# Seven slots instead of eight for the exponentials, a flat fan-out of the reciprocals, and the output bias added by TensorE, in a fused attention and feed-forward kernel

## The chip, the cores and the metric

The program runs on the 8 cores of one Trainium2 chip. Cores 2b and 2b+1 share batch b: each owns 2048 of its 4096 rows and reads the other 2048 for keys and values. The cores don't talk to each other. The metric is the device time of the slowest core, in microseconds (us). Before the change it was 1568.64 us, the median of three runs (1566.05 to 1570.06).

## The reference

```python
x = x + attention(layernorm(x), query_proj, key_proj, value_proj, output_proj)   # x: 4 x 4096 x 1024
x = x + ffn(layernorm(x), Win, bin_, W1, b1, W2, b2, Wout, bout)

# attention: 16 query heads of 64, one key head and one value head shared by all
q = einsum('bnd,hkd->bnhk', r, query_proj); k = r @ key_proj; v = r @ value_proj
attn = softmax(q k / sqrt(64)); out = einsum('bnhv,dhv->bnd', attn v, output_proj)

# ffn, 64 narrow units of inner width 16
s = x @ Win + bin_;  h = relu(s[..., None] * W1 + b1);  g = sum(h * W2) + b2;  out = g @ Wout + bout
```

## The kernel before

Five queues of instructions, one for each engine, are filled by calls of `S.emit` in program order; each call names the semaphore values that it waits for. The order of these calls is the order on each engine. A wait that the same engine has already passed is not repeated.

**Stage A** (the first 262 us) loads weights, normalises 32 tiles of 128 rows, transposes them and makes keys `k2t`, values `vab` and queries `qt`.

**Stage B** is attention. It goes through 1024 groups in one row: 4 blocks k of 512 queries, in each 8 pairs of heads, in each 32 chunks `mc` of 128 keys. For a group TensorE makes the scores of both heads (`s_pair`, line 479: two matmuls, one on array rows 0 to 63 and one on 64 to 127) into one of two PSUM buffers `spa` and `spb`, ScalarE takes the exponential of all 128x1024 of them into a slot of `ptu` (line 494), and TensorE multiplies four quarters of it with the values (line 518, here called PV). In turn `it` of the loop the queues get: the exponential of group `it`; the scores of group `it + 2`; and four PV matmuls, into `oAe` for group `it - 5`, `oAo` for `it - 4`, `oBe` for `it - 3` and `oBo` for `it - 2`. So the last reader of a group's slot runs in the turn five later. The scores of a group wait for the exponential of the group two before, which frees their PSUM buffer. `pvT[g]` is the semaphore value that the last PV of turn `g + 2` gives.

With eight slots, the slot of group g was last read in turn g - 3. The scores of group g come later than that on TensorE's queue, so the exponential's wait for its own scores covers it, and there is no other wait.

At the end of each pair of heads VectorE copies `oBo` and `oAo` to `big` (line 533) and adds `oBe` and `oAe` (line 536). The ones column of `vab` gives the softmax sums, gathered in `zstage`. At the end of a block k the sums of 16 heads are inverted (line 566) and written to DRAM as 64 copies of a 16x512 table, `zscr`: SyncE writes four copies (line 572), then doubles them four times, 4 to 8 to 16 to 32 to 64 (line 576), each doubling waiting for the one before. GpSimd reads 64 copies of a head's row into 64 partitions (`rcpb`, line 587), and VectorE multiplies (`emit_zmult`, line 432). For blocks 0 to 2 these products are queued on VectorE in the pairs of heads of the next block, from the 11th chunk of each; for the last block they stand at the start of stage C.

**Stage C** projects the heads (`op_ps`, line 733), adds x (line 708), spills the sum to DRAM (`x2d`, line 753), normalises and transposes. After every fourth tile `emit_D` does the feed-forward of 512 rows: eight rounds of Relu and multiply-add, then for each of four tiles `fo = g2b @ wout2b` (line 659), a load of the spilled tile (`big<-x2d`, line 667), their sum (line 670), the bias (line 678) and two half stores (line 682). There is one `fo`. SyncE's queue holds load, store, store, load, store, store, so a load stands behind the stores of the tile before it.

Of the kernel before, what the change touches and what calls it, by code (L numbers as in the profile page):

```python
# [7 lines left out]
F32 = mybir.dt.float32  # L8
BF16 = mybir.dt.bfloat16
AF = mybir.ActivationFunctionType  # L10
# [12 lines left out]
EPS = 1e-5  # L23

ENGS = ("sync", "tensor", "vector", "scalar", "gpsimd")
SEMS = ("pe", "dve", "act", "xa", "xb", "xc", "xd", "g", "zg", "zs", "zs2", "zs3", "zs4", "out", "ou2", "ou3", "ou4", "wd", "od", "zh", "pl", "x2r")
DMA_SEMS = {"xa", "xb", "g", "zg", "zs", "out"}


# [55 lines left out]
def build_nc(debug=False, upto='D'):  # L85
# [4 lines left out]
    nc = bass.Bass("TRN2", target_bir_lowering=False)  # L90
# [38 lines left out]
    st = contextlib.ExitStack()  # L129
    with st:  # L130
# [7 lines left out]
        boutbc = st.enter_context(nc.sbuf_tensor("boutbc_s", [128, D], F32))  # L138
        stats = st.enter_context(nc.sbuf_tensor("stats", [128, 8, 4], F32))
        w1p = st.enter_context(nc.sbuf_tensor("w1p_s", [128, 8], F32))  # L140
        b1p = st.enter_context(nc.sbuf_tensor("b1p_s", [128, 8], F32))
        b1adj = st.enter_context(nc.sbuf_tensor("b1adj", [128, 8], F32))
        w2p = st.enter_context(nc.sbuf_tensor("w2p_s", [128, 8], F32))
        bin2 = st.enter_context(nc.sbuf_tensor("bin2_s", [128, 1], F32))
        b2h = st.enter_context(nc.sbuf_tensor("b2h_s", [128, 1], F32))
# [5 lines left out]
        wout2b = st.enter_context(nc.sbuf_tensor("wout2b", [128, D], BF16))  # L151
        identb = st.enter_context(nc.sbuf_tensor("identb", [128, 128], BF16))
        k2t = st.enter_context(nc.sbuf_tensor("k2t", [128, NFULL], BF16))
        vab = st.enter_context(nc.sbuf_tensor("vab", [128, MC, 65], BF16))
        qt = st.enter_context(nc.sbuf_tensor("qt", [128, DCH, NOWN], BF16))
        ot = st.enter_context(nc.sbuf_tensor("ot", [128, DCH, NOWN], BF16))
        r1t = st.enter_context(nc.sbuf_tensor("r1t", [128, 2, DCH, NTW], BF16))
        ptu = st.enter_context(nc.sbuf_tensor("ptu", [128, 8, 1024], BF16))
        r1u = st.enter_context(nc.sbuf_tensor("r1u", [128, 2, D], BF16))
        g2b = st.enter_context(nc.sbuf_tensor("g2b", [128, NTW], BF16))  # L160

# [2 lines left out]
        S = Sched(block, sems)  # L164
# [5 lines left out]
        def x2dbuf(q):  # L170
            return big[:, 4096 + q * 1024: 4096 + (q + 1) * 1024]
        def obuf(q):
            return big[:, 6144 + q * 1024: 6144 + (q + 1) * 1024]
# [93 lines left out]
        for dsrc, ddst in direct:  # L267
# [73 lines left out]
        for step in range(NTILES + 3):  # L341
# [4 lines left out]
            if i < NTILES:  # L346
                q = i % 4
# [14 lines left out]
            if 0 <= i < NTILES:  # L362
                q, qr = i % 4, i % 2
# [8 lines left out]
            if 0 <= i < NTILES:  # L372
# [4 lines left out]
                    waits=[("pe", trans_t[i]), ("pe", slabmm_t.get(i // 4 - 2, 0))], inc="dve")  # L377
# [28 lines left out]
        sp = [spa, spb]  # L406
# [45 lines left out]
        sPT = {}  # L452
        pvT = {}
# [33 lines left out]
        for it in range(-2, NG + PVLAG):  # L487
            gmc = it
            if 0 <= gmc < NG:
                ew = [("pe", sPT[gmc])]  # L490
                if first_act:
                    ew += bwB["scalar"]
                    first_act = False
                expT[gmc] = S.emit("scalar", lambda s_, gmc=gmc: s_.activation(  # L494
                    ptu[:, gmc % 8, :], sp[gmc % 2][:], AF.Exp, scale=0.125),
                    waits=ew, inc="act")
            gmc = it + 2
            if 0 <= gmc < NG:
# [8 lines left out]
            for oi in range(4):  # L507
# [8 lines left out]
                if mc == 0:  # L516
                    w_i.append(("dve", tcfree.get((hp - 1, oi), 0)))
                tgt = S.emit("tensor", lambda te, ob=ob, rg=rg, col=col, mc=mc, gmc=gmc: te.matmul(  # L518
                    ob[:], vab[rg:rg + 64, mc, :], ptu[rg:rg + 64, gmc % 8, col:col + 512],
                    start=(mc == 0), stop=(mc == MC - 1)),  # L520
                    waits=w_i, inc="pe" if (oi == 3 or mc == MC - 1) else None)
                if oi == 3:
# [24 lines left out]
            if 0 <= gmc < NG:  # L547
                k, j, mc = gmc // (NHP * MC), (gmc // MC) % NHP, gmc % MC
                hp = gmc // MC
                if mc == MC - 1:  # L550
                    tg = None
                    if j == NHP - 1 and KHP == NHP and os.environ.get("KNTEND") != "0":
# [18 lines left out]
                        for cc in range(4):  # L571
                            tzo = S.emit("sync", lambda e, cc=cc: e.dma_start(zscr[cc], recipz[:]),
                                         waits=tzw if cc == 0 else (), inc="zh", inc_n=16)
                        for dd in range(2, 6):
                            lo, hi = 1 << dd, 1 << (dd + 1)
                            tzo = S.emit("sync", lambda e, lo=lo, hi=hi: e.dma_start(
                                zscr[lo:hi], zscr[0:lo]),
                                waits=[("zh", tzo)], inc="zh", inc_n=16)

                        def emit_bcast(kk, i_, tzo=tzo):  # L580
                            zst = zstate[kk]
# [34 lines left out]
        r2evac_t = {}  # L616
        tfa_t = {}
        out_r = out_d.rearrange("(t p) d -> t p d", p=128)
        spill_t = {}
        r2norm_t = {}  # L620
        relu_t = {}
# [6 lines left out]
        def emit_D(k):  # L628
# [25 lines left out]
            for ns in range(4):  # L654
                t = k * 4 + ns
                q = ns % 2
                fw = [("dve", tg2b), ("dve", fadd_t.get(t - 1, 0))]
                for half in range(2):
                    fo_mm_t[t] = S.emit("tensor", lambda te, ns=ns, half=half: te.matmul(  # L659
                        fo[:, half * 512:(half + 1) * 512], g2b[:, ns * 128:(ns + 1) * 128],  # L660
                        wout2b[:, half * 512:(half + 1) * 512], start=True, stop=True),
                        waits=fw if half == 0 else (), inc="pe" if half == 1 else None)
                sm = "wd" if t % 2 == 0 else "x2r"
                osems = ("out", "ou3") if t % 2 == 0 else ("ou2", "ou4")
                xw = [("g", spill_t[t]), ("dve", tfa_t.get(t - 2, 0)),
                      ("dve", multT.get((KL, HEADS - 1), 0))]
                txl = S.emit("sync", lambda e, t=t, q=q: e.dma_start(
                    x2dbuf(q), x2d.rearrange("(t p) d -> t p d", p=128)[t]),
                    waits=xw, inc=sm, inc_n=16)
                tfa = S.emit("vector", lambda v, q=q: v.tensor_tensor(  # L670
                    obuf(q), x2dbuf(q), fo[:], op=ALU.add),
                    waits=[("pe", fo_mm_t[t]), (sm, txl),
                           (osems[0], outdma_t.get((t - 2, 0), 0)),
                           (osems[1], outdma_t.get((t - 2, 1), 0)),
                           ("dve", multT.get((KL, HEADS - 1), 0))],
                    inc="dve")
                tfa_t[t] = tfa
                fadd_t[t] = S.emit("vector", lambda v, q=q: v.tensor_tensor(  # L678
                    obuf(q), obuf(q), boutbc[:], op=ALU.add),
                    waits=[("dve", tfa)], inc="dve")  # L680
                for h in range(2):
                    outdma_t[(t, h)] = S.emit("sync", lambda e, t=t, q=q, h=h: e.dma_start(
                        out_r[t, :, h * 512:(h + 1) * 512], obuf(q)[:, h * 512:(h + 1) * 512]),
                        waits=[("dve", fadd_t[t])] if h == 0 else (), inc=osems[h], inc_n=16)

        KL = KNT - 1
        for step in range(16 + 4):
# [146 lines left out]
```

How the kernel before makes its waits and increments, by code:

```python
            def body(e, items=items):  # L74
                for waits, fn, inc, inc_n in items:
                    for s, v in waits:
                        e.wait_ge(self.sems[s], v)
                    r = fn(e)
                    if inc is not None:
                        r.then_inc(self.sems[inc], inc_n)
```

## Time and profile before

| | |
|---|---|
| median of three runs | 1568.64 us |
| the profiled execution | 1568.78 us |
| its span, slowest core (0) | 1567.2 us |
| spans of the 8 cores | 1551.0 to 1567.2 us |
| ScalarE busy | 1104.5 us (70%) |
| TensorE busy, matmul | 1097.0 us (70%) |
| VectorE busy | 358.9 us (23%) |
| mean granted clock of TensorE, core 0 | 0.88 |

The span is what lies between the first and the last instruction of the program on the slowest core. The granted clock is 1 at 2.4 GHz and 0.5 at 1.2 GHz. Matmul ends are modelled, and busy times of pipelined instructions overlap, so a busy share near 1 doesn't mean that an engine works at its peak. A name such as `DMA zscr<-zscr` in the chain is a transfer from its issue to its landing.

### The profile page before, as it was taken

Reading aid. Unit: us, or ns where it says so; the run is one execution under the profiler, and the core shown is the slowest. Engines: PE = TensorE matmul, PEld = TensorE weight load, DVE = VectorE, ACT = ScalarE, POOL = GpSimd, SP = SyncE. Lnnn points to the kernel's source line nnn. Section 1 sums busy time; section 2 is a strip of 40 time slices with the busy share of each in tenths; the row PEclk is TensorE's granted clock in tenths of the full one; section 3 lists DMA queues with packets and bytes.
Section 4 is the critical chain, followed back from the end, with each engine's and each line's share of the span. In section 5 each row is a group of like instructions: output and inputs, shape, how many; then the busy total and the mean of one; then the engine's idle time right before and its main releaser. Section 6 shows DMA issues by size and latency. Waiting matters only on the chain.

```text
span 1567.2 us, 20849 instructions; the slowest of 8 cores (1551.0 to 1567.2 us)
## 1 busy us (share of the span) xinstructions
PE 1097.0 (70%) x7407; PEld 417.6 (27%) x7424; DVE 358.9 (23%) x663; ACT 1104.5 (70%) x1347; POOL 94.8 (6%) x188
## 2 busy tenths in 40 slices
PE   0376646999999889999899999889999345253421
PEld 0233322333333233333333333333333112021110
DVE  2344443101001211211211111121121134343443
ACT  0523354999999899999899999989999214040310
POOL 0000000000000100100110000010000030000000
PEclk9987766999999999999999999999999768575755
DMA  5311232100000200000200000200000142325132
GB/s 163 121 56 57 82 111 82 43 1 1 1 1 1 85 10 10 18 3 3 77 18 10 9 12 3 62 27 16 10 10 4 54 144 98 129 86 178 63 134 94
DMA packets 30227, 81.74 MB, mean 52 GB/s; under 512 B 9264, under 2 KB 10288, under 8 KB 29872
## 3 DMA queue, kind: packets, MB, share of 16 engines
q1 hardware_dynamic: 21424, 60.87, 11.9%
q0 software_dynamic: 8704, 19.54, 3.9%
q8 instruction: 63, 1.03, 0.3%
q14 instruction: 36, 0.29, 0.1%
HBM read 60.34 MB, written 25.17 MB: 55 GB/s over the span
## 4 chain that ended last, share of the span: by engine, by line
ACT 43%; PE 19%; DMA 16%; issue 11%; DVE 9%; SPq 1%; DVEq 0%; POOL 0%; ACTq 0%; POOLq 0%
ACT ptu L494 37%; DMA zscr<-zscr 4%; DMA x2d<-big 4%; PE qps L332 4%; DMA big<-x2d 3%; PE spa L479 3%; PE oAe L518 3%; PE oBe L518 3%; PE spb L479 2%; ACT big L189 2%; ACT big L185 2%; PE kps L305 2%; DMA ot<-r1u 1%; DVE big L678 1%; DVE big L670 1%
## 5 line engine op out<-in xcount | busy, mean ns | idle before, releaser
L494 ACT ACTIVATE ptu<-spb 128x1024 bf16<-128x1024 f32 x512 | 568.6, 1110 | 15.2 <-PE spb L479 14.7
L494 ACT ACTIVATE ptu<-spa 128x1024 bf16<-128x1024 f32 x512 | 569.6, 1113 | 1.5 <-PE spa L479 1.4
L518 PE MATMUL oBo<-ptu,vab 64*65 64x512 bf16 x1024 | 389.2, 380 | 14.9 <-DVE big L533 12.4
L518 PE MATMUL oAo<-ptu,vab 64*65 64x512 bf16 x1024 | 387.9, 379 | 2.5 <-DVE big L533 0.5
L518 PE MATMUL oBe<-ptu,vab 64*65 64x512 bf16 x1024 | 386.9, 378 | 1.4
L518 PE MATMUL oAe<-ptu,vab 64*65 64x512 bf16 x1024 | 384.8, 376 | 2.0 <-DVE big L536 0.4
L479 PE MATMUL spa<-qt,k2t 64*128 64x512 bf16 x1024 | 205.0, 383 | 48.3 <-ACT ptu L494 6.3
L479 PE MATMUL spb<-qt,k2t 64*128 64x512 bf16 x1024 | 211.0, 383 | 38.8 <-ACT ptu L494 0.5
L533 DVE COPY big<-oBo 65x512 f32<-65x512 f32 x32 | 22.0, 687 | 722.5 <-PE oBo L518 722.2
L202 ACT ACTIVATE stats<-stats,epsb 128x1 f32<-128x1 f32 x48 | 14.1, 294 | 225.9 <-DVE stats L200 225.9
L518 PEld LDWEIGHTS oBe<-ptu,vab 64*65 64x65 bf16 x1024 | 108.7, 106 | 98.0 <-issue 14.7
L479 PEld LDWEIGHTS spa<-qt,k2t 64*128 64x128 bf16 x1024 | 65.0, 93 | 254.5 <-issue 251.7
L479 PEld LDWEIGHTS spb<-qt,k2t 64*128 64x128 bf16 x1024 | 65.5, 93 | 242.9 <-issue 239.9
L220 PE MATMUL trpsA<-identb,r1u 128*128 128x128 bf16 x256 | 30.1, 291 | 135.2 <-DVE r1u L210 135.2
L518 PEld LDWEIGHTS oAo<-ptu,vab 64*65 64x65 bf16 x1024 | 119.6, 117 | 17.9 <-issue 17.7
L518 PEld LDWEIGHTS oBo<-ptu,vab 64*65 64x65 bf16 x1024 | 110.8, 108 | 29.7 <-issue 29.6
L518 PEld LDWEIGHTS oAe<-ptu,vab 64*65 64x65 bf16 x1024 | 106.8, 104 | 20.0 <-issue 16.2
L733 PE MATMUL op_ps<-wq_wp,ot 128*128 128x512 bf16 x248 | 77.4, 477 | 47.9 <-DVE ot L432 35.3
L659 PE MATMUL fo<-wout2b,g2b 128*128 128x512 bf16 x32 | 16.2, 608 | 101.2 <-DVE big L678 67.0
L540 POOL DMA_DIRECT2D zstage<-big x64 | 31.7, 496 | 813.7 <-DVE big L536 745.4
L185 ACT ACT_TABLE_LOAD x2 | 2.6, 1283 | 96.3 <-DVE ot L432 53.8
L220 PEld LDWEIGHTS trpsA<-identb,r1u 128*128 128x128 bf16 x256 | 22.9, 130 | 142.6 <-issue 142.6
(63 smaller groups left out, 778.0 us busy)
## 6 DMA issues: line engine op xcount, KB each, us to landing
xbuf<-x_own SPq DMA_DIRECT2D x32, 512.0 KB, 3.6
xbuf<-x_oth SPq DMA_DIRECT2D x16, 512.0 KB, 3.3
rcpb<-zscr POOLq DMA_DIRECT2D x64, 128.0 KB, 2.7
x2d<-big POOLq DMA_DIRECT2D x16, 512.0 KB, 2.9
big<-x2d SPq DMA_DIRECT2D x16, 512.0 KB, 4.1
out<-big SPq DMA_DIRECT2D x32, 256.0 KB, 2.3
xbuf<-wq SPq DMA_DIRECT2D x8, 512.0 KB, 4.3
xbuf<-wp SPq DMA_DIRECT2D x8, 512.0 KB, 4.2
```

Of the source, the lines that this page charges most:

```text
L185: "scalar", lambda s, a=xt_ap, dmp=dmp, c=sc: s.activation(dmp, a, AF.Square, accum_out=stat(SUMSQ, c)),
L189: "scalar", lambda s, a=xt_ap, dmp=dmp, c=sc: s.activation(dmp, a, AF.Identity, accum_out=stat(SUMS, c)),
L220: t = S.emit("tensor", lambda te, jj=jj, h=half: te.transpose(trps[:, h * 1024 + jj * 128: h * 1024 + (jj + 1) * 128], src_ap_fn(jj), iden ...
L305: t = S.emit("tensor", lambda te, j=j: te.matmul(kps[:], wkb[:, j, :], R1T[:, j, :], start=(j == 0), stop=(j == DCH - 1)), waits=mmw if j ...
L332: t = S.emit("tensor", lambda te, j=j, c=c: te.matmul(qps[:, c % 2, :], wq_wp[:, j, c * 128:(c + 1) * 128], R1T[:, j, :], start=(j == 0), ...
L479: tgt = S.emit("tensor", lambda te, mc=mc, rg=rg, hh=hh, j=j, k=k: te.matmul(sp[gmc % 2][:, hh * 512:(hh + 1) * 512], k2t[rg:rg + 64, mc * ...
L494: expT[gmc] = S.emit("scalar", lambda s_, gmc=gmc: s_.activation(ptu[:, gmc % 8, :], sp[gmc % 2][:], AF.Exp, scale=0.125), waits=ew, inc=" ...
L518: tgt = S.emit("tensor", lambda te, ob=ob, rg=rg, col=col, mc=mc, gmc=gmc: te.matmul(ob[:], vab[rg:rg + 64, mc, :], ptu[rg:rg + 64, gmc % ...
L533: tcfree[(hp, oi)] = S.emit("vector", lambda v, hi=hi, hh=hh: v.tensor_copy(tv(hi)[0:65, :], obank[2 * hh + 1][:]), waits=tw, inc="dve")
L540: tg = S.emit("gpsimd", lambda e, hi=hi: e.dma_start(zstage[hi:hi + 1, :], tv(hi)[64:65, :]), waits=[("dve", tc)] + (bwB["gpsimd"] if hp = ...
L659: fo_mm_t[t] = S.emit("tensor", lambda te, ns=ns, half=half: te.matmul(fo[:, half * 512:(half + 1) * 512], g2b[:, ns * 128:(ns + 1) * 128] ...
L733: tmm = S.emit("tensor", lambda te, t=t, half=half, c=c: te.matmul(op_ps[:, t % 2, half * 512:(half + 1) * 512], ot[:, c, t * 128:(t + 1) ...
```

## The change

Four edits:

1. `ptu` has seven slots. The exponential of group g now waits as well for `pvT[g - 4]`, the last PV of turn g - 2.
2. The fan-out of `zscr`: after the four first copies, 15 transfers of four copies each, all from the first four, with one wait ahead of the first. The bytes are the same.
3. The bias goes into `fo` on TensorE: after each half's bf16 matmul one of a [1, 128] row of ones with the fp32 bias row. VectorE's bias addition is gone, the stores wait for the sum of line 670, and the next tile's `fo` waits for that too.
4. The load of the spilled tile is cut into two halves with a semaphore each.

```diff
-        ptu = st.enter_context(nc.sbuf_tensor("ptu", [128, 8, 1024], BF16))
+        ptu = st.enter_context(nc.sbuf_tensor("ptu", [128, 7, 1024], BF16))
+        S.emit("vector", lambda v: v.memset(ones1[:], 1.0))
...
-                ew = [("pe", sPT[gmc])]
+                ew = [("pe", sPT[gmc]), ("pe", pvT.get(gmc - 4, 0))]
...
-                        for dd in range(2, 6):
-                            lo, hi = 1 << dd, 1 << (dd + 1)
-                            tzo = S.emit("sync", lambda e, lo=lo, hi=hi: e.dma_start(
-                                zscr[lo:hi], zscr[0:lo]),
-                                waits=[("zh", tzo)], inc="zh", inc_n=16)
+                        seed = tzo
+                        for rr in range(1, 16):
+                            tzo = S.emit("sync", lambda e, rr=rr: e.dma_start(
+                                zscr[4 * rr:4 * rr + 4], zscr[0:4]),
+                                waits=[("zh", seed)] if rr == 1 else (), inc="zh", inc_n=16)
...
-                fw = [("dve", tg2b), ("dve", fadd_t.get(t - 1, 0))]
+                fw = [("dve", tg2b), ("dve", tfa_t.get(t - 1, 0))]
...
-                        wout2b[:, half * 512:(half + 1) * 512], start=True, stop=True),
-                        waits=fw if half == 0 else (), inc="pe" if half == 1 else None)
+                        wout2b[:, half * 512:(half + 1) * 512], start=True, stop=False),
+                        waits=fw if half == 0 else ())
+                    fo_mm_t[t] = S.emit("tensor", lambda te, half=half: te.matmul(
+                        fo[:, half * 512:(half + 1) * 512], ones1[:],
+                        boutbc[0:1, half * 512:(half + 1) * 512], start=False, stop=True),
+                        inc="pe" if half == 1 else None)
...
-                txl = S.emit("sync", lambda e, t=t, q=q: e.dma_start(
-                    x2dbuf(q), x2d.rearrange("(t p) d -> t p d", p=128)[t]),
-                    waits=xw, inc=sm, inc_n=16)
+                for h in range(2):
+                    txl[h] = S.emit("sync", lambda e, t=t, q=q, h=h: e.dma_start(
+                        x2dbuf(q)[:, h * 512:(h + 1) * 512],
+                        x2d_r[t, :, h * 512:(h + 1) * 512]),
+                        waits=xw if h == 0 else (), inc=rsems[h], inc_n=16)
...
-                fadd_t[t] = S.emit("vector", lambda v, q=q: v.tensor_tensor(
-                    obuf(q), obuf(q), boutbc[:], op=ALU.add),
-                    waits=[("dve", tfa)], inc="dve")
...
-                        waits=[("dve", fadd_t[t])] if h == 0 else (), inc=osems[h], inc_n=16)
+                        waits=[("dve", tfa)] if h == 0 else (), inc=osems[h], inc_n=16)
```

In stage B no instruction changes its place. This is TensorE's queue after the change, one turn of the loop and the start of the next (`L481` is the scores' line, `L520` that of PV, both two lines lower than before):

```order
L481 MATMUL spa<-qt,k2t 128x512 [waits sem_act]
L481 MATMUL spa<-qt,k2t 128x512
L520 MATMUL oAe<-ptu,vab 65x512
L520 MATMUL oAo<-ptu,vab 65x512
L520 MATMUL oBe<-ptu,vab 65x512
L520 MATMUL oBo<-ptu,vab 65x512
L481 MATMUL spb<-qt,k2t 128x512 [waits sem_act]
```

The exponential that reads `spa` waited for the second of these rows; now it waits for the sixth.

SyncE's queue at the end of block 0, before (`recipz` is the table of inverted sums):

```order
L572 DMA zscr<-recipz 16x512 [waits sem_dve]
L572 DMA zscr<-recipz 16x512 x3
L576 DMA zscr<-zscr 16x2048 [waits sem_zh]
L576 DMA zscr<-zscr 16x4096 [waits sem_zh]
L576 DMA zscr<-zscr 16x8192 [waits sem_zh]
L576 DMA zscr<-zscr 16x16384 [waits sem_zh]
```

And after:

```order
L574 DMA zscr<-recipz 16x512 [waits sem_dve]
L574 DMA zscr<-recipz 16x512 x3
L578 DMA zscr<-zscr 16x2048 [waits sem_zh]
L578 DMA zscr<-zscr 16x2048 x14
```

Four waits have become one, and four transfers 15 of the smallest size.

TensorE's queue for two tiles of `emit_D` after the change (`L662` is what was line 659, `L666` the bias; `ones` is the row of ones):

```order
L662 MATMUL fo<-wout2b,g2b 128x512 [waits sem_dve]
L666 MATMUL fo<-boutbc_s,ones 128x512
L662 MATMUL fo<-wout2b,g2b 128x512
L666 MATMUL fo<-boutbc_s,ones 128x512
L662 MATMUL fo<-wout2b,g2b 128x512 [waits sem_dve]
```

A tile had two matmuls here and has four; the wait of the last row is now for the sum of the tile before, no longer for the bias addition behind it.

## Rows read from the trace of the kernel before

**Rows 1.** The exponentials into one buffer: duration ns min/median/max, first and last start us.
```profile
L494 ACT ACTIVATE ptu<-spb x512: 1017/1106/1197, 264.9 to 1224.9; 128x1024 bf16<-128x1024 f32 x171
```

**Rows 2.** Timeline, one turn in steady state: start us, us, engine, line, op, tiles, count.
```profile
799.21 1.03 ACT L494 ACTIVATE ptu<-spa 128x1024 bf16<-128x1024 f32 x1
...
800.38 0.39 PE L479 MATMUL spa<-qt,k2t 64*128 64x512 bf16 x2
...
800.83 0.38 PE L518 MATMUL oBo<-ptu,vab 64*65 64x512 bf16 x1
...
801.02 1.05 ACT L494 ACTIVATE ptu<-spa 128x1024 bf16<-128x1024 f32 x1
```

**Rows 3.** Timeline, start of stage B, at the lower clock; in brackets idle time and releaser.
```profile
268.90 0.61 PE L479 MATMUL spa<-qt,k2t 64*128 64x512 bf16 x2
...
269.73 0.63 PE L518 MATMUL oBo<-ptu,vab 64*65 64x512 bf16 x1
269.82 0.97 PE L479 MATMUL spb<-qt,k2t 64*128 64x512 bf16 x2
...
270.89 1.02 ACT L494 ACTIVATE ptu<-spb 128x1024 bf16<-128x1024 f32 x1 [0.26 <-PE spb L479]
```

**Rows 4.** Timeline where block 1's first pair of heads ends.
```profile
533.52 1.20 ACT L494 ACTIVATE ptu<-spa 128x1024 bf16<-128x1024 f32 x1
536.10 0.68 DVE L432 TENSOR_TENSOR ot<-big,rcpb 64x512 bf16<-64x512 f32 x1 [23.31 <-DMA rcpb<-zscr]
...
537.49 0.69 DVE L533 COPY big<-oBo 65x512 f32<-65x512 f32 x1
538.32 0.60 PE L518 MATMUL oBo<-ptu,vab 64*65 64x512 bf16 x1 [4.49 <-DVE big L533]
...
539.45 1.02 ACT L494 ACTIVATE ptu<-spb 128x1024 bf16<-128x1024 f32 x1 [4.73 <-PE spb L479]
```

**Rows 5.** Chain of waits after the last block: start us, us, what.
```profile
1238.81 4.08 DMA zscr<-zscr
...
1249.72 7.65 DMA zscr<-zscr
...
1257.91 2.68 DMA rcpb<-zscr
```

**Rows 6.** Timeline, the four tiles of the first feed-forward block.
```profile
1337.24 1.01 PE L659 MATMUL fo<-wout2b,g2b 128*128 128x512 bf16 x2 [8.53 <-DVE g2b L652]
1338.43 1.22 DVE L670 TENSOR_TENSOR big<-big,fo 128x1024 f32<-128x1024 f32 x1 [1.33 <-PE fo L659]
...
1341.05 0.82 SPq L682 DMA_DIRECT2D out<-big  x2
...
1341.96 0.41 SPq L667 DMA_DIRECT2D big<-x2d  x1
1346.06 1.22 DVE L670 TENSOR_TENSOR big<-big,fo 128x1024 f32<-128x1024 f32 x1 [5.08 <-DMA big<-x2d]
...
1361.87 1.22 DVE L670 TENSOR_TENSOR big<-big,fo 128x1024 f32<-128x1024 f32 x1 [5.20 <-DMA big<-x2d]
...
1364.33 0.81 DVE L210 TENSOR_SCALAR ptu<-big,stats 128x1024 bf16<-128x1024 f32 x1
```

**Rows 7.** The page's DMA issues: queue, count, size of each, median us to landing.
```profile
big<-x2d SPq DMA_DIRECT2D x16, 512.0 KB, 4.1
out<-big SPq DMA_DIRECT2D x32, 256.0 KB, 2.3
```

**Rows 8.** Stretches: window, length, busy us of each engine, granted clock, DMA share, GB/s.
```profile
1319.80:1333.50 13.70, 7.51 (x39) 3.25 (x38) 7.05 (x14) 9.31 (x16) 0.53 (x1) 1.00 0.10 39
...
1333.50:1371.00 37.50, 9.76 (x28) 3.15 (x29) 13.97 (x18) 2.40 (x5) 0.53 (x1) 0.50 0.40 132
...
800.00:1000.00 200.00, 180.37 (x1300) 63.64 (x1296) 29.73 (x41) 199.60 (x218) 14.32 (x28) 1.00 0.03 9
```

More of the change, by code:

```diff
@@ L25 @@
 ENGS = ("sync", "tensor", "vector", "scalar", "gpsimd")
-SEMS = ("pe", "dve", "act", "xa", "xb", "xc", "xd", "g", "zg", "zs", "zs2", "zs3", "zs4", "out", "ou2", "ou3", "ou4", "wd", "od", "zh", "pl", "x2r")
+SEMS = ("pe", "dve", "act", "xa", "xb", "xc", "xd", "g", "zg", "zs", "zs2", "zs3", "zs4", "out", "ou2", "ou3", "ou4", "wd", "od", "zh", "pl", "x2r", "x2b", "x2c")
 DMA_SEMS = {"xa", "xb", "g", "zg", "zs", "out"}
@@ L142, in build_nc @@
         b1adj = st.enter_context(nc.sbuf_tensor("b1adj", [128, 8], F32))
+        ones1 = st.enter_context(nc.sbuf_tensor("ones1", [1, 128], F32))
         w2p = st.enter_context(nc.sbuf_tensor("w2p_s", [128, 8], F32))
@@ L494, in build_nc @@
                 expT[gmc] = S.emit("scalar", lambda s_, gmc=gmc: s_.activation(
-                    ptu[:, gmc % 8, :], sp[gmc % 2][:], AF.Exp, scale=0.125),
+                    ptu[:, gmc % 7, :], sp[gmc % 2][:], AF.Exp, scale=0.125),
                     waits=ew, inc="act")
@@ L518, in build_nc @@
                 tgt = S.emit("tensor", lambda te, ob=ob, rg=rg, col=col, mc=mc, gmc=gmc: te.matmul(
-                    ob[:], vab[rg:rg + 64, mc, :], ptu[rg:rg + 64, gmc % 8, col:col + 512],
+                    ob[:], vab[rg:rg + 64, mc, :], ptu[rg:rg + 64, gmc % 7, col:col + 512],
                     start=(mc == 0), stop=(mc == MC - 1)),
@@ L618, in build_nc @@
         out_r = out_d.rearrange("(t p) d -> t p d", p=128)
+        x2d_r = x2d.rearrange("(t p) d -> t p d", p=128)
         spill_t = {}
@@ L656, in emit_D @@
                 q = ns % 2
-                fw = [("dve", tg2b), ("dve", fadd_t.get(t - 1, 0))]
+                fw = [("dve", tg2b), ("dve", tfa_t.get(t - 1, 0))]
                 for half in range(2):
-                    fo_mm_t[t] = S.emit("tensor", lambda te, ns=ns, half=half: te.matmul(
+                    S.emit("tensor", lambda te, ns=ns, half=half: te.matmul(
                         fo[:, half * 512:(half + 1) * 512], g2b[:, ns * 128:(ns + 1) * 128],
-                        wout2b[:, half * 512:(half + 1) * 512], start=True, stop=True),
-                        waits=fw if half == 0 else (), inc="pe" if half == 1 else None)
-                sm = "wd" if t % 2 == 0 else "x2r"
+                        wout2b[:, half * 512:(half + 1) * 512], start=True, stop=False),
[4 more added lines that the diff above has]
+                        inc="pe" if half == 1 else None)
+                rsems = ("wd", "x2b") if t % 2 == 0 else ("x2r", "x2c")
                 osems = ("out", "ou3") if t % 2 == 0 else ("ou2", "ou4")
@@ L666, in emit_D @@
                       ("dve", multT.get((KL, HEADS - 1), 0))]
-                txl = S.emit("sync", lambda e, t=t, q=q: e.dma_start(
-                    x2dbuf(q), x2d.rearrange("(t p) d -> t p d", p=128)[t]),
-                    waits=xw, inc=sm, inc_n=16)
+                txl = {}
+                for h in range(2):
[3 more added lines that the diff above has]
+                        waits=xw if h == 0 else (), inc=rsems[h], inc_n=16)
                 tfa = S.emit("vector", lambda v, q=q: v.tensor_tensor(
                     obuf(q), x2dbuf(q), fo[:], op=ALU.add),
-                    waits=[("pe", fo_mm_t[t]), (sm, txl),
+                    waits=[("pe", fo_mm_t[t]), (rsems[0], txl[0]), (rsems[1], txl[1]),
                            (osems[0], outdma_t.get((t - 2, 0), 0)),
```

## The prediction

> **What bounds the kernel now.** I read first the page's busy shares, which name no engine (ScalarE and TensorE 70% each), then the exponentials' own row, which gives the length of stage B, then the timeline of one turn, then the chain of waits for what lies behind stage B, and the timeline of one feed-forward block. The reader is to see in them three places with different limits.
>
> In stage B the 512 exponentials into `spb` start from 264.9 to 1224.9 us [rows 1]: 1022 steps of one exponential in 960.0 us, 0.939 us each. The 1023 steps from the first to the last of all make 960.9 us, stalls at block ends included. In steady state ScalarE works at its own rate: two exponentials later the next one into `spa` starts 1.81 us on (799.21 to 801.02), that is one each 0.905 us, with no idle time shown [rows 2]. The scores it needs ended at 800.38 + 0.39 = 800.77, before its start. But the last PV behind those scores ended at 800.83 + 0.38 = 801.21, after its start. With eight slots nobody minds. This is the comparison on which the forecast rests.
>
> At the ends of blocks there is a stall: VectorE waits 23.31 us for `rcpb`, the copy of `oBo` queued behind it is late, TensorE waits 4.49 us, and between two exponentials lie 5.93 us (533.52 to 539.45) instead of 0.92 [rows 4]. It comes with each of three blocks, so 3 x 5.0 = 15 us of the 960.9. After the last block the doublings run alone: from 1238.81 to 1249.72 + 7.65 = 1257.37, 18.6 us [rows 5]. In the feed-forward blocks the loop is sum, bias, two stores issued, load issued behind them, landing, sum [rows 6].
>
> **Edit 1, seven slots.** The exponential of a group must now wait for the last PV of the turn in which its scores were made. That closes a cycle over two groups: exponential, scores, four PV, exponential. From the rows: an exponential that starts behind a wait takes 1.02 us (the minimum of rows 1 is 1017 ns, and rows 3 have 1.02 after a wait). From its end to the start of the next scores into the same buffer, 799.21 + 1.03 = 800.24 to 800.38, are 0.14 us; from there to the end of the last PV, 801.21, are 0.83 [rows 2]. From the end of a matmul to an exponential that waited for it, 269.82 + 0.97 = 270.79 to 270.89, are 0.10 [rows 3]. Sum 2.09 us for two exponentials, 1.045 each. The two cycles (even and odd groups) share the engines without harm: ScalarE needs 0.905 of 1.045, and TensorE's 0.83 fits too. 1023 x 1.045 = 1069.0 us.
>
> Where a pair of heads ends, the first `oBo` of the next pair waits for VectorE's copy. From the end of the last one: 0.10, the copy 0.69, and 538.32 - 538.18 = 0.14 to TensorE's start [rows 4], together 0.93; at a pace of 1.045 and a matmul of 0.38 it would start 0.67 later by itself. So 0.26 is late, now on the cycle: 31 crossings, 8 us. The same crossings before are within the 960.9. Stage B after: 1077 us, 116 more. The stalls at block ends are taken as gone from it: the first pair of a block lasts 32 x (1.045 - 0.92) = 4.0 us longer, which nearly covers the 4.49 alone, and edit 2 brings the reciprocals sooner. Bounds of the pace: if the modelled matmul ends are 0.1 late, 0.995 (51 us less); if the second wait on ScalarE costs 0.05 each time, 1.07 (26 us more).
>
> **Edit 2, flat fan-out.** The 15 transfers are issued one behind the other: two issues of stores with what is between them take 1341.96 - 1341.05 = 0.91 us [rows 6], 0.455 each. The last is issued 14 x 0.455 = 6.4 us after the first and lands 4.08 later, like the first doubling of the same 128 KB [rows 5]: 10.5 us instead of 18.6. Worth 8 us behind the last block. Bounds: all 1.92 MB at the rate of the last doubling (1 MB in 7.65 us) is 14 us, gain 4.6; landing in 2.3 [rows 7], 8.7 us, gain 10.
>
> The Trainium skill speaks against this edit: "DMA: Bandwidth & Descriptors", section Bandwidth, wants transfers of 1 MiB or more and gives 0.95 us for 64 KB against 6.15 for 1 MB. By it 15 pieces would take over 14.3 us and gain at most a few, so the kernel would come out some 5 us later than my sum.
>
> **Edits 3 and 4, feed-forward blocks.** A block now takes 1337.24 to 1364.33, 27.1 us [rows 6]. The bias addition goes: from the last sum to what follows it are 2.46 us, less the sum's 1.22, so 1.24 each time. The step from one tile's sum to the next becomes: sum to store 1341.05 - 1338.43 - 1.24 = 1.38, stores' issue 0.91, then the load. That now takes 1346.06 - 1341.96 = 4.10. In halves it is bounded below by 0.455 + 2.3 = 2.8 (a half store's landing, rows 7) and above by 0.455 + 4.1 = 4.6; the bytes and the queue behind the stores are the same, so I stay near the present row and take 3.9. Step 6.2, three of them 18.6.
>
> The bias matmul is in no row. Below, it costs as much as its bf16 neighbour at the same clock: the pair takes 1.01 [rows 6], a single 0.61 [rows 3], so 0.40. Above I put 2.44, two fp32 additions of a tile on VectorE, the dearest pass over such data here. Nearest is the bf16 matmul; with twice the bytes I take 0.8. Two of them delay each block's first sum by 1.6 us. On the other three tiles they lie beside the load: TensorE's path from sum to sum is 1.22 + 0.14 + 1.01 + 0.10 plus two bias matmuls, 4.1 us, against 6.2. The cover ends at 1.85 us for one. A block: 1.19 + 1.6 + 18.6 + 1.2 = 22.6 us, 4.5 less; four blocks, 18 us.
>
> "FP8 and Floating Point Precision", section TensorE Precision Notes, in the Trainium skill says that a true fp32 product takes four passes through the array. By it a bias matmul would take 1.6 us at this clock, still under cover on three tiles, and the sum would rise by 4 x 1.6 = 6 us; no run here shows it yet.
>
> **Sum**, against the profiled execution's 1568.78 us (its span 1567.2, the median of the runs 1568.64, so the same thing): 1568.8 + 116 - 8 - 18 = 1659; I say 1660.
>
> **Rivals.**
> *The wait is met anyway, and the kernel gets faster.* Place: the exponential's start. It costs nothing if the real end of the PV is at least 801.21 + 0.10 - 801.02 = 0.29 us earlier than modelled. For it: the ends are modelled, and ScalarE's recorded starts run a little ahead (durations creep from 1.02 to 1.20). Against it: in rows 2 the duration is 1.05, so only 0.03 of the start is ahead. Then only the gains stay: 1568.8 - 15 - 8 - 18 = 1528.
> *The clock falls.* TensorE idles more. At the lower clock scores to last PV take 268.90 to 269.73 + 0.63 = 270.36, 1.46 us [rows 3], so 2.72 for two, 1.36 each: 1982 us if always, 1820 if half the time. Against it: the clock stayed at 1.00 over 13.7 us in which TensorE was 55% busy and fell only in a stretch of 26%; steady state is at 90% [rows 8], and would be at 0.83 / 1.045 = 79%.
> *The bias matmuls become the bound.* At 2.44 us each, TensorE's step is 7.4 against today's 7.8 and the first sum is 4.9 late: a block takes 29.4 us, 2.3 more than today. 1660 + 18 + 9 = 1687.
> *Half the wait shows*, matmul ends 0.1 late: 1609.
>
> **How the numbers follow.** The forecast's case 0.80, bias matmuls bound 0.08, wait met 0.05, half the wait 0.04, clock 0.03. The forecast's own bounds are the pace (1.02 to 1.07: 25 us either way), the fan-out (3) and the blocks (8). Range 1630 to 1695, which takes in the bias case and leaves out the rest, with a tenth of the main case. Faster by over 0.3% (what a measurement of this kernel can tell from none, 5 us) 0.05, within it 0.01, slower 0.94.
>
> **What would show it.** In the changed profile: steps of 1.03 to 1.06 us between exponentials, durations at 1.02 without creep, idle time before each of them, released by the PV line; TensorE's granted clock near 1.00 in all of stage B; no 5 us hole at block ends; about 10.5 us from the first copy of `zscr` to the last landing; in a feed-forward block about 6.2 us from sum to sum, with the load, not `fo`, last. I am wrong if exponentials still step by 0.92, if the clock shows stretches of 0.5 in stage B, or if `fo` is what the sums wait for.

## The result and the profile after

The changed kernel takes 1696.26 us, the median of 9 runs, against 1568.45 for the kernel before (10 runs). The ratio is 1.081, 95% interval 1.076 to 1.085: 8% slower, 128 us. Ratios, here and below, leave out executions in which the cores of one die showed a lower granted clock and a longer span; medians take in all executions. The direction, the place and the mechanism of the slowdown are those of the forecast, but 1696 lies 36 us above the 1660 that I predicted and 1 us outside the range of 1630 to 1695. The forecast for the feed-forward blocks had the wrong sign.

The profiled execution took 1693.96 us, its slowest core (5) has a span of 1692.2. These are the exponentials of the changed kernel, in the form of [rows 1] (duration ns min/median/max, first and last start us):

```profile
L496 ACT ACTIVATE ptu<-spa x512: 1017/1019/1025, 265.4 to 1352.2; 128x1024 bf16<-128x1024 f32 x171
L496 ACT ACTIVATE ptu<-spb x512: 1017/1024/1025, 266.3 to 1353.4; 128x1024 bf16<-128x1024 f32 x171
```

From the first to the last are 1088.0 us, where [rows 1] give 960.9, so stage B is 127 us longer, where the spans differ by 125 in all. The durations no longer creep up to 1.20: each exponential starts behind a wait.

The timeline of steady state answers to [rows 2]:

```profile
801.00 1.02 ACT L496 ACTIVATE ptu<-spa 128x1024 bf16<-128x1024 f32 x1
...
802.17 0.39 PE L481 MATMUL spa<-qt,k2t 64*128 64x512 bf16 x2
802.17 1.02 ACT L496 ACTIVATE ptu<-spb 128x1024 bf16<-128x1024 f32 x1
...
802.38 0.37 PE L520 MATMUL oAe<-ptu,vab 64*65 64x512 bf16 x1
...
802.62 0.38 PE L520 MATMUL oBo<-ptu,vab 64*65 64x512 bf16 x1
803.09 1.02 ACT L496 ACTIVATE ptu<-spa 128x1024 bf16<-128x1024 f32 x1
```

The next exponential into `spa` is 803.09 - 801.00 = 2.09 us later: end of the exponential 802.02, scores 802.17, end of the last PV 803.00, exponential 803.09. That is the predicted cycle, each term within 0.01. The two cycles stand unevenly to each other. From 801.00 to 802.17, `spa` to `spb`, are 1.17 us, and from 802.17 to 803.09, `spb` to `spa`, are 0.92. The page shows idle time mostly ahead of the `spb` ones (75.5 us in all, against 17.0), so the sign "idle time before each of them" held for one buffer only; both start 0.09 us after the last PV that they wait for. In the middle 20 groups of a head pair the mean step is 1.0445 us.

These rows also show that the wait is later than the slot needs. The slot that group g takes over was last read by `oAe` of turn g - 2, the first of the four PV, but the kernel sets a semaphore only behind the fourth, `oBo`. `oAe` ends at 802.38 + 0.37 = 802.75, 0.25 us before `oBo`. A wait for `oAe` alone would make the cycle about 1.84 us, 0.92 for one exponential; that is an estimate from these rows, and no run tested it.

Where a head pair ends, two matmuls are late by 0.4 us, each held by VectorE (in brackets idle time and releaser):

```profile
369.39 1.02 ACT L496 ACTIVATE ptu<-spa 128x1024 bf16<-128x1024 f32 x1
...
370.57 0.69 DVE L535 COPY big<-oBo 65x512 f32<-65x512 f32 x1 [30.12 <-PE oBo L520]
...
370.98 0.37 PE L520 MATMUL oBe<-ptu,vab 64*65 64x512 bf16 x1
371.40 0.37 PE L520 MATMUL oBo<-ptu,vab 64*65 64x512 bf16 x1
...
371.87 1.02 ACT L496 ACTIVATE ptu<-spa 128x1024 bf16<-128x1024 f32 x1 [0.29 <-PE oBo L520]
...
372.79 1.02 ACT L496 ACTIVATE ptu<-spb 128x1024 bf16<-128x1024 f32 x1
...
373.74 0.68 DVE L538 TENSOR_TENSOR big<-big,oAe 65x512 f32<-65x512 f32 x1 [0.61 <-PE oAe L520]
...
374.56 0.37 PE L520 MATMUL oAe<-ptu,vab 64*65 64x512 bf16 x1 [0.21 <-DVE big L538]
...
375.28 1.02 ACT L496 ACTIVATE ptu<-spb 128x1024 bf16<-128x1024 f32 x1 [0.30 <-PE oBo L520]
```

`oBo` starts 0.42 after `oBe` and not 0.02, and the exponential behind it comes 2.48 us after the last one of its buffer (369.39 to 371.87); three turns later `oAe` does the same to the other buffer (372.79 to 375.28). 32 groups take 34.04 us instead of 32 x 1.0445 = 33.42, so the two together cost 0.62.

The holes of [rows 4] are gone; the 32 groups in which they lay take 34.0 us like any others. TensorE's clock stays full in stage B at 79% busy, as was argued, and is at the lower level in the feed-forward blocks (columns as in [rows 8]):

```profile
800.00:1000.00 200.00, 157.65 (x1127) 54.12 (x1128) 27.15 (x37) 182.63 (x188) 17.40 (x34) 1.00 0.09 24
1463.00:1483.00 20.00, 15.03 (x18) 3.60 (x18) 3.66 (x3) 0.00 (x0) 0.00 (x0) 0.50 0.46 157
```

The first feed-forward block answers to [rows 6]:

```profile
1458.62 0.59 PE L662 MATMUL fo<-wout2b,g2b 128*128 128x512 bf16 x1 [8.53 <-DVE g2b L655]
1459.14 2.07 PE L666 MATMUL fo<-boutbc_s,ones 1*128 1x512 f32 x2
1461.14 0.61 PE L662 MATMUL fo<-wout2b,g2b 128*128 128x512 bf16 x1
1461.68 2.07 PE L666 MATMUL fo<-boutbc_s,ones 1*128 1x512 f32 x2
1463.99 1.22 DVE L680 TENSOR_TENSOR big<-big,fo 128x1024 f32<-128x1024 f32 x1 [5.51 <-PE fo L666]
1465.29 0.81 SPq L689 DMA_DIRECT2D out<-big  x2
...
1466.19 0.90 SPq L676 DMA_DIRECT2D big<-x2d  x2
...
1470.73 1.22 DVE L680 TENSOR_TENSOR big<-big,fo 128x1024 f32<-128x1024 f32 x1 [5.52 <-PE fo L666]
```

One bias matmul is two records and lasts 2.07 us in all. `fo` takes 5.1 us a tile instead of 1.0, and the releaser in the brackets has changed from the load in [rows 6] to `PE fo`. The step from sum to sum is 6.74 us here, and the first sum comes 5.4 us after the first `fo` begins instead of 1.2. The block is 27.0 us long, [rows 6] make it 27.1. `fo` is not last everywhere: of the 96 such steps on the eight cores it ends the wait of 63, with a mean step of 6.86 us, and the load ends that of 33, with 7.26.

The fan-out on SyncE's queue, and how it landed in the chain of waits:

```profile
1367.07 9.34 SPq L578 DMA_DIRECT2D zscr<-zscr  x15
```

```profile
1371.52 0.57 SPq L578
...
1375.84 3.05 DMA zscr<-zscr
```

The issues take 9.34 us, 0.62 each, and 11.8 us pass from the first to the last landing; [rows 5] give 18.6.

The difference of the two spans, 1692.2 - 1567.2 = 125.0 us: stage B + 127.1, its start + 1.4, the fan-out - 6.7, the four feed-forward blocks + 3.6 (112.4 against 108.8 from first `fo` to the end of the last sum or bias), the rest - 0.4.

### The profile page after: what moved, and what is told of

Its sections match the earlier page's. It is cut to its first block, busy times and chain, and to the rows that moved or that the text cites. A ratio compares the mean times of both kernels' runs of the same rounds, so it can differ in the third digit from the quotient of the medians.

```text
span 1692.2 us, 22047 instructions; the slowest of 8 cores (1685.6 to 1692.2 us)
## 1 busy us (share of the span) xinstructions
PE 1165.2 (69%) x7488; PEld 423.8 (25%) x7488; DVE 339.2 (20%) x648; ACT 1155.6 (68%) x1347; POOL 94.5 (6%) x188
## 4 chain that ended last, share of the span: by engine, by line
PE 38%; ACT 34%; issue 10%; DMA 8%; DVE 7%; SPq 1%; ACTq 1%; DVEq 0%; POOL 0%; POOLq 0%
ACT ptu L496 29%; PE spb L481 10%; PE oAe L520 7%; PE oBe L520 6%; PE qps L334 3%; DMA x2d<-big 3%; PE fo L666 3%; ACT big L190 2%; ACT big L186 2%; PE oBo L520 2%; PE spa L481 2%; PE kps L307 2%; DMA ot<-r1u 1%; DVE big L680 1%; DMA xbuf<-wq 1%
## 5 line engine op out<-in xcount | busy, mean ns | idle before, releaser
L496 ACT ACTIVATE ptu<-spb 128x1024 bf16<-128x1024 f32 x512 | 524.2, 1024 | 75.5 <-PE oBo L520 15.7
L496 ACT ACTIVATE ptu<-spa 128x1024 bf16<-128x1024 f32 x512 | 521.9, 1019 | 17.0 <-PE oBo L520 13.6
L520 PE MATMUL oBo<-ptu,vab 64*65 64x512 bf16 x1024 | 386.5, 377 | 2.9
L520 PE MATMUL oAe<-ptu,vab 64*65 64x512 bf16 x1024 | 382.4, 374 | 5.3 <-DVE big L538 5.3
L520 PE MATMUL oAo<-ptu,vab 64*65 64x512 bf16 x1024 | 386.0, 377 | 0.0
L520 PE MATMUL oBe<-ptu,vab 64*65 64x512 bf16 x1024 | 383.9, 375 | 0.2 <-DVE big L538 0.2
L481 PE MATMUL spb<-qt,k2t 64*128 64x512 bf16 x1024 | 202.2, 381 | 162.4 <-ACT ptu L496 158.9
L481 PE MATMUL spa<-qt,k2t 64*128 64x512 bf16 x1024 | 201.9, 381 | 61.7 <-ACT ptu L496 19.0
L481 PEld LDWEIGHTS spb<-qt,k2t 64*128 64x128 bf16 x1024 | 64.0, 93 | 384.6 <-issue 384.6
L481 PEld LDWEIGHTS spa<-qt,k2t 64*128 64x128 bf16 x1024 | 64.1, 93 | 285.7 <-issue 285.6
L520 PEld LDWEIGHTS oBe<-ptu,vab 64*65 64x65 bf16 x1024 | 108.4, 106 | 97.7 <-issue 13.6
L520 PEld LDWEIGHTS oAo<-ptu,vab 64*65 64x65 bf16 x1024 | 119.7, 117 | 1.7 <-issue 0.2
L520 PEld LDWEIGHTS oBo<-ptu,vab 64*65 64x65 bf16 x1024 | 110.4, 108 | 17.2 <-issue 17.2
L520 PEld LDWEIGHTS oAe<-ptu,vab 64*65 64x65 bf16 x1024 | 106.2, 104 | 13.7 <-issue 13.1
L666 PE MATMUL fo<-boutbc_s,ones 1*128 1x512 f32 x64 | 66.2, 1136 | 0.0
L662 PE MATMUL fo<-wout2b,g2b 128*128 128x512 bf16 x32 | 19.1, 596 | 58.1 <-DVE g2b L655 34.1
```

The lines of the kernel that those rows point to most:

```text
L481: tgt = S.emit("tensor", lambda te, mc=mc, rg=rg, hh=hh, j=j, k=k: te.matmul(sp[gmc % 2][:, hh * 512:(hh + 1) * 512], k2t[rg:rg + 64, mc * ...
L666: fo_mm_t[t] = S.emit("tensor", lambda te, half=half: te.matmul(fo[:, half * 512:(half + 1) * 512], ones1[:], boutbc[0:1, half * 512:(half ...
```

## The experiments

Ratios are to runs of the kernel before on the same chip. Three experiments ran on another chip than the others: edits 2 to 4 with the bf16 bias, the load ahead, and the short copies. The table's last four columns are medians over the cores whose records are complete, from the profiled execution of each kernel: first to last exponential; first `zscr<-zscr` transfer to last landing after the last block; first `fo` to the normalisation behind a feed-forward block, mean of three blocks; mean step from sum to sum. Where no added wait holds stage B, its length differs by 5 to 9 us between the cores of one execution, so a few us in that column between such kernels tell nothing.

| kernel | median us | ratio, 95% interval | stage B | fan-out | block | step |
|---|---|---|---|---|---|---|
| before | 1568 to 1570 | | 959.8 | 15.9 | 26.7 | 7.68 |
| changed | 1696.3 | 1.081 (1.076 to 1.085) | 1088.1 | 12.7 | 27.6 | 6.95 |
| edit 1 alone | 1697.4 | 1.078 (1.073 to 1.084) | 1087.9 | 16.0 | 26.4 | 7.57 |
| edits 2 to 4, eight slots | 1561.4 | 0.994 (0.991 to 0.996) | 948.3 | 14.6 | 27.6 | 6.98 |
| the same, wait kept | 1695.5 | 1.078 (1.073 to 1.083) | 1087.8 | 12.6 | 27.6 | 6.94 |
| changed, PV first | 1561.2 | 0.993 (0.990 to 0.995) | 952.1 | 14.3 | 27.8 | 6.99 |
| edit 2 alone | 1553.5 | 0.989 (0.984 to 0.995) | 948.2 | 14.4 | 26.2 | 7.48 |
| edits 3 and 4 alone | 1574.2 | 1.002 (0.999 to 1.005) | 957.9 | 15.0 | 27.9 | 7.05 |
| edits 2 and 3 | 1557.6 | 0.991 (0.987 to 0.994) | 949.5 | 14.3 | 27.2 | 6.89 |
| edits 2 and 3, bf16 bias | 1540.4 | 0.981 (0.976 to 0.987) | 952.8 | 14.5 | 22.3 | 6.29 |
| edits 2 to 4, bf16 bias | 1549.2 | 0.984 (0.979 to 0.989) | 948.7 | 14.2 | 23.4 | 6.55 |
| edit 2, bf16 bias, load ahead | 1509.9 | 0.960 (0.955 to 0.965) | 950.8 | 14.3 | 15.4 | 3.92 |

**Edit 1 alone**, on the kernel before:

```diff
-        ptu = ... [128, 8, 1024]
+        ptu = ... [128, 7, 1024]
-                ew = [("pe", sPT[gmc])]
+                ew = [("pe", sPT[gmc]), ("pe", pvT.get(gmc - 4, 0))]
```

> The kernel before with edit 1 alone (seven slots, exponential of group g waits for the last PV of turn g - 2). Theory (the cycle exponential, scores, four PV, exponential sets the pace, 2.09 us for two groups, and each change of head pair adds 0.6): the exponentials run from first to last in 1088 us as in the changed kernel, the feed-forward blocks stay at 27.1 us, the stall at block ends shrinks from 5 us to under 1 though the doublings stay: 1695 us, or 1 to 2 more. Rival A (my predicted stage B of 1077 us was right for edit 1, and the 11 us more come from the other edits' traffic): 1684. Rival B (the slow pace needs the other edits): near 1568.

Measured 1697.4 us with stage B at 1088. These are its exponentials, on the slowest core:

```profile
L494 ACT ACTIVATE ptu<-spb x512: 1017/1024/1025, 264.9 to 1352.9; 128x1024 bf16<-128x1024 f32 x171
```

The whole slowdown is edit 1's, rivals A and B fall. The block-end holes shrink to 0.5 us at most although the doublings stay: the slower pace covers them, as predicted.

**Edit 1 undone**:

```diff
-                ew = [("pe", sPT[gmc]), ("pe", pvT.get(gmc - 4, 0))]
+                ew = [("pe", sPT[gmc])]
...
+            if k == 0:
+                S.emit("vector", lambda v: v.memset(zstage[0:1, 0:128], 1.0),
+                       waits=[("dve", trec0[0])])
```

> The changed kernel with eight slots and no added wait; the row of ones for the bias stands in a corner of zstage, since SBUF has no room for both. Theory: stage B falls to the pace of 0.92, first to last exponential 946 us (the block-end stalls stay away because the flat fan-out is 4.6 us shorter), so 1696 - 142 = 1554 us: edits 2 to 4 together gain 14, all from the fan-out and none from the feed-forward blocks. Rival (edits 3 and 4 gain the 18 us that I predicted once stage B is out of the way): 1536. Rival (block-end stalls stay): 1566.

Stage B came back nearly as expected (945.8 us on the slowest core, 948.3 in the median). The total is 1561, between the expected 1554 and the 1566 of the rival in which the block-end holes stay, and far from 1536. The trace shows the holes partly there: on the four cores that begin stage B first each still costs about 1 to 4 us. The other edits bring 8 us, none of it from the feed-forward blocks, which are about 1 us longer each than before.

**Eight slots, wait kept**: as the run above, with the wait left in.

> The changed kernel with eight slots but the added wait kept, which eight slots do not need. Theory (the wait is the cost, not where the slots lie): same as the changed kernel, 1696 us, pace 1.045. Rival (with seven slots the addresses of readers and writer collide or the slot order matters): nearer to 1554.

1695.5 us and 1087.8, the changed kernel again. Eight slots don't help an exponential that waits as if there were seven; the wait is the cost.

**PV ahead of the scores**: the changed kernel with seven slots and the wait, but the four PV are queued first:

```diff
-            gmc = it + 2
-            if 0 <= gmc < NG:
-                ...
-                s_pair(gmc)
             outs = [(oAe, 0, 0), (oAo, 64, 0), (oBe, 0, 512), (oBo, 64, 512)]
             for oi in range(4):
                 ...
+            gmc = it + 2
+            if 0 <= gmc < NG:
+                ...
+                s_pair(gmc)
```

> The changed kernel, seven slots and the added wait, but in each turn the four PV matmuls are queued ahead of the scores of group it + 2. Theory (the place of the PV in the cycle is the cost): the wait is over before the scores are, the cycle is 1.02 + 0.14 + 0.39 + 0.10 = 1.65 us for two, under ScalarE's own 1.83, so the pace returns to 0.92: about 1554 us, up to 1562 if head pair changes now delay the scores. Rival (any wait of ScalarE on PV costs the same): 1696. Rival (PV ahead of the scores delays these behind it): above 1600.

1561.2 us, the same as with eight slots. The timeline of this kernel in steady state:

```profile
799.86 1.13 ACT L496 ACTIVATE ptu<-spa 128x1024 bf16<-128x1024 f32 x1
...
800.67 0.38 PE L511 MATMUL oBo<-ptu,vab 64*65 64x512 bf16 x1
800.77 1.14 ACT L496 ACTIVATE ptu<-spb 128x1024 bf16<-128x1024 f32 x1
801.14 0.39 PE L481 MATMUL spa<-qt,k2t 64*128 64x512 bf16 x2
...
801.67 1.16 ACT L496 ACTIVATE ptu<-spa 128x1024 bf16<-128x1024 f32 x1
```

The last PV ends at 801.05, before the scores of its turn begin (801.14) and long before the exponential that waits for it (801.67). Over these rows the step is 0.905, as in [rows 2], in the middle of the head pairs it is 0.915 (0.914 before), and durations creep as they do before the change. So not the slot and not the wait as such, but what TensorE has to do between the scores and the last PV. This is the experiment that shows the mechanism.

**Edit 2 alone**, on the kernel before:

> The kernel before with edit 2 alone (15 parallel copies instead of four doublings). Theory: the fan-out takes 12 to 14.5 us instead of 16.5 to 18.5, because one issue on SyncE costs 0.61 us and not the 0.455 that I took; the stalls at three block ends go from 5 us to about 0.5, and 4 us are gained behind the last block: 1569 - 14 - 4 = 1551 us. Rival (the flat fan-out is worth only what lies behind the last block): 1565. Rival (many small transfers are no faster than one large): 1569.

1553.5 us, near the expected 1551. The split came out otherwise. The holes at block ends don't close on the slowest core: each of the three keeps 2 to 3 of its 5 us (32 groups take 31.4, 32.4 and 31.6 us instead of 29.6). It is much the same on all four cores that begin stage B at 259 to 260 us; on the four that begin it at 264 to 266 the first two holes are under 1 us and the third keeps 2 to 3. Why these differ is open. Stage B is 12 us shorter in the median, and behind the last block the cores gain 1.5 us in the median (15.9 to 14.4).

**Edits 3 and 4 alone**:

> The kernel before with edits 3 and 4 (fp32 bias matmuls in fo, load in halves), eight slots and the doublings as before. Theory (one bias matmul takes two records of 1.03 us each, 2.1 us, over the 1.85 at which its cover ends, so TensorE sets the step from sum to sum and each block's first sum is 4.1 us later): a feed-forward block takes 27.5 to 29.5 us instead of 27.1, total 1569 plus 2 to 10 us, about 1577. Rival (my sum, 4.5 us less for each block): 1551.

1574.2 us; the interval, 0.999 to 1.005, holds no change as well as the 5 us more. What it excludes is my sum of 18 us less. The step fell by 0.6 us, the bias addition's 1.2 being half eaten, and the first sum of each block is 4 us later: 27.9 against 26.7. Both waits are at work: of 96 steps `fo` ends 47, at 6.86 us, and the load 49, at 7.40.

**Load in one piece**, fp32 bias, eight slots and no added wait:

```diff
-                    txl[h] = S.emit("sync", lambda e, t=t, q=q, h=h: e.dma_start(
-                        x2dbuf(q)[:, h * 512:(h + 1) * 512], ...
+                txl = S.emit("sync", lambda e, t=t, q=q: e.dma_start(
+                    x2dbuf(q), x2d_r[t]), ...
```

> The changed kernel with eight slots, no added wait and the spilled tile's load in one piece again (edits 2 and 3 alone). Theory: the load is not what the sums wait for, so this is the same as with halves, 1561 us, within 3. Rival (two transfers in flight disturb each other and the stores, and the halves cost the extra us in the feed-forward blocks): 1553.

1557.6 against 1561.4 us, 3.8 less where I expected at most 3. The intervals overlap and the steps differ by 0.1, so this neither shows nor excludes a small cost of the halves. In the traces of the eight cores the load ends 16 of 96 steps in one piece and 32 in halves; `fo` ends the rest. So mostly the load isn't what the sums wait for, and the halves make it so more often.

**Load in one piece, bias in bf16**: as above and

```diff
+                S.emit("vector", lambda v: v.memset(k2t[0:1, 1024:1152], 1.0))
+                S.emit("vector", lambda v: v.tensor_copy(k2t[0:1, 0:1024], boutbc[0:1, :]))
...
-                        fo[:, half * 512:(half + 1) * 512], ones1[:],
-                        boutbc[0:1, half * 512:(half + 1) * 512], start=False, stop=True),
+                        fo[:, half * 512:(half + 1) * 512], k2t[0:1, 1024:1152],
+                        k2t[0:1, half * 512:(half + 1) * 512], start=False, stop=True),
```

> As the run before this one, and the bias row and the row of ones in bf16 (in two unused corners of k2t), so that the bias is rounded to bf16. Theory (the fp32 matmul is what ate the gain of edit 3): one bias matmul takes 0.41 us, the step from sum to sum is again set by stores, load and landing at 6.5 us, a block takes 23 us instead of 28, total 1561 - 20 = 1541 us. Rival (the load behind the stores is the bound in both, so nothing changes): 1560.

1540.4 us, 17 less than with fp32, and the block falls from 27.2 to 22.3. The timeline:

```profile
1329.48 0.60 PE L667 MATMUL fo<-k2t 1*128 1x512 bf16 x1
...
1330.02 0.61 PE L663 MATMUL fo<-wout2b,g2b 128*128 128x512 bf16 x1
...
1334.04 1.22 DVE L678 TENSOR_TENSOR big<-big,fo 128x1024 f32<-128x1024 f32 x1 [5.22 <-DMA big<-x2d]
```

A bias matmul holds the next one by about 0.53 us (1329.48 to 1330.02), and the load ends the wait of all 96 sums behind the first of a block. The block is near the 22.6 us that I had forecast, with the load last and a step of 6.29 for 6.2; the forecast was for an fp32 bias at 0.8 us, and only a cheaper one gives it.

**The same with the load in halves**:

> The changed kernel with eight slots, no added wait, the bias in bf16 and the spilled tile's load in two halves. Against the same with one load (1540 us). Theory: the load is now what the sums wait for, and the second half is issued 0.45 us after the first while the bytes are the same, so it lands no sooner: 1540 to 1546 us. Rival (halves land sooner, as edit 4 is built for): 1533 or less.

1549.2 us, intervals overlapping with the run before. The cores' traces differ more clearly: step 6.55 against 6.29, block 23.4 (23.1 to 23.9 over the cores) against 22.3 (22.1 to 22.6). So edit 4 seems to cost about 0.3 us a step where the load is the bound. It is one profiled execution of each, on different chips.

**Load ahead of the stores**: bf16 bias, one piece, and `big<-x2d` of tile t + 1 is queued before the stores of tile t:

```diff
+            txls = {0: load_x2(0)}
             for ns in range(4):
                 ...
+                if ns < 3:
+                    txls[ns + 1] = load_x2(ns + 1)
                 tfa = S.emit("vector", ...
```

> As the run with the bf16 bias and one load, and the load of the next tile is queued on SyncE ahead of the stores of this one. Theory (the step is the serial path sum, stores' issue, load's issue, landing): the load of a tile now needs only the sum two tiles back, the step from sum to sum falls from 6.5 us to about 4, bounded by TensorE's 3.5 and by the transfers; 12 steps save 30 us: 1510 us. Rival (the transfers share 16 engines and a megabyte each tile is the bound): step over 5.5, 1530.

1509.9 us. Timeline:

```profile
1327.09 1.22 DVE L687 TENSOR_TENSOR big<-big,fo 128x1024 f32<-128x1024 f32 x1 [2.51 <-PE fo L678]
1328.38 0.81 SPq L696 DMA_DIRECT2D out<-big  x2
...
1329.28 0.40 SPq L664 DMA_DIRECT2D big<-x2d  x1
...
1330.82 1.22 DVE L687 TENSOR_TENSOR big<-big,fo 128x1024 f32<-128x1024 f32 x1 [2.51 <-PE fo L678]
...
1334.69 1.22 DVE L687 TENSOR_TENSOR big<-big,fo 128x1024 f32<-128x1024 f32 x1 [2.65 <-PE fo L678]
```

The load issued at 1329.28 serves the sum at 1334.69, not the one at 1330.82. The step is 3.9 us, set by the sum and TensorE's four bf16 matmuls; `fo` ends 89 of 96 steps, so the transfers were not the bound. This version beats both kernels, 4% under the one before.

**Short copies**, on the changed kernel: at a head pair's end VectorE handles 64 of 512 columns, in the copies and in the additions (not shown below). The kernel leaves out seven eighths of the attention output, and it serves only to time the rest. There is one execution, 1681.35 us.

```diff
...
-                        tv(hi)[0:65, :], obank[2 * hh + 1][:]), waits=tw, inc="dve")
+                        tv(hi)[0:65, 0:64], obank[2 * hh + 1][:, 0:64]), waits=tw, inc="dve")
```

> The changed kernel, but at each end of a head pair VectorE copies and adds 64 of the 512 columns (the rest of big holds ones from a memset ahead of stage A, so most of the output is left out of the computation). Theory (the excess at each change of head pair, 34.04 us for 32 groups against 32 x 1.0445 = 33.42, is the two late matmuls oBo and oAo of one parity, each held by a 0.69 us copy): a copy takes about 0.2 us, nothing is late, 33.4 us for 32 groups and 1069 us from the first to the last exponential instead of 1088. Rival (the excess has to do with semaphores or the first matmul into a bank): stays at 34.0.

The copy takes 0.22 us, 32 groups mostly 33.4 and up to 33.7, and stage B 1071.4 us (core 7) instead of 1088.0. So 17 of the 19 us of excess at head pair changes are due to the length of VectorE's copies and additions; the rival, 34.0, falls.

## Why the prediction was right and wrong

*That the added wait closes a cycle and sets stage B's pace*: right. 2.09 us for two groups was predicted and measured, the step is 1.0445 for 1.045. Shown by edit 1 alone, by the kept wait with eight slots, and by the PV put first.

*"31 crossings, 8 us"*: mis-sized, the smaller part of the miss. Measured (34.04 - 33.42) x 31 = 19 us. I set the path of 0.93 us (copy and both hand-overs) against the mean step. But the two cycles alternate 0.92 and 1.17, and after the short step the matmul is 0.39 late, not 0.26. And I followed one held matmul where there are two, `oBo` and `oAe`. The short copies take away 17 of these 19 us. The term came out 11 us too small.

*The holes at block ends go*: right, for the first reason given (the slower pace), which edit 1 alone shows. The second reason would not have done it: with edit 2 alone about half of each hole stays on the slowest core.

*Fan-out, gain 8*: 6.7 between the slowest cores. The size rests on one core's 18.6 us, while the median of the cores is 15.9; and one issue takes 0.62 us, not the 0.455 that I carried over from stores. The batching rule of the Trainium skill ("DMA: Bandwidth & Descriptors", section Bandwidth), by which, as I worked it out, the small transfers would gain at most a few us, fits the median of the cores with edit 2 alone (1.5 us) better than my sum does. Most of edit 2's 15 us came from the block ends inside stage B, 12 us, to which I had given nothing of edit 2 because the slower pace hides them.

*"with twice the bytes I take 0.8"*: the step that failed, and the larger part of the miss. The 0.8 doubled a bf16 price that I took as 0.40, the pair's 1.01 less 0.61. That 0.61 of [rows 3] is a row of two scores matmuls on different array rows and not a single one; the number hardly suffered, since a single `fo` matmul is recorded at 0.59 to 0.61. But doubling for the bytes had no row behind it. A bias matmul takes 2.07 us, above the 1.85 at which I had put the end of its cover. So TensorE, and not the load, ends most waits and sets the step (6.95 instead of 6.2), and each first sum is 4.2 us late instead of 1.6. That `fo` is what the sums wait for was one of the prediction's own signs of being wrong. The four blocks came out 3.6 us longer instead of 18 shorter: 21.6 us. The rival "the bias matmuls become the bound" had the mechanism, at a chance of 0.08, and its price for the blocks (9 longer) was nearer than mine. The Trainium skill's four passes for a true fp32 product ("FP8 and Floating Point Precision", section TensorE Precision Notes), set beside the sum at 1.6 us, was the better guide: the trace shows two records and not four, but their 2.07 us are four times the 0.53 that a bf16 one adds here. Even 1.6 would have been under the cover, so by that rule too the blocks would have gained.

*Load in halves, 3.9 instead of 4.1*: wrong in sign as far as the traces tell, though small. Where the load is the bound the step with halves is 0.26 us longer.

Put together: 1659 + 11 + 21.6 + 1.3 (fan-out) + 1.4 (stage B's later start) - 0.4 (rest) = 1693.9, against 1693.96 of the profiled execution. That execution lies inside the range and the median 1.3 us outside, so the near miss says little; the blocks' sum was off by 22 us.

*Not settled*: why the fan-out after the last block takes 12.7 us where stage B is slow and 14.3 where it is fast, with the same transfers; what edits 3 and 4 alone cost, which is within 0.5% of nothing; and whether seven slots would cost anything at all if the exponential waited for `oAe` alone.

## What to carry to other kernels

When a buffer ring loses a slot, look which queue entry the new wait names and what stands in front of that entry on its engine: the wait costs the whole way round the loop, and moving the reader ahead of the next producer can make it free (seven slots with PV first took 1561.2 us, eight slots 1561.4). Look too whether the entry that sets the semaphore is the one that reads the slot last. Work put on an engine because it idles has to be priced by the operand's type at the clock that the idling engine has there. And a load queued behind the stores of the tile before it is a serial path, however little the transfer engines are used: moving it ahead was worth about 30 us (1540.4 to 1509.9), more than any of the four edits gained.

## What the runs showed of the hardware

An fp32 matmul of 512 columns with a one-row contraction takes 2.07 us in two records at 1.2 GHz; a bf16 one of the same shape adds 0.53. Fifteen DRAM-to-DRAM transfers of 128 KB issued one behind the other on SyncE's queue start 0.62 us apart, stores of 256 KB 0.45. Recorded durations of ScalarE tell whether it is held: behind a wait every exponential of 128x1024 lasts 1.02 us, while without one the duration creeps from 1.02 to 1.20 though the starts stay 0.91 apart.
